# Two-layer graph network on one core: one-run picks, two-input compares, and no small reduces on VectorE

## The reference, cut to what matters

```python
# x (6250, 64), 200000 edges: src, dst (sorted), edge_attr (200000, 64), edge_weight
h = max(layernorm(x), 0)
hw = h @ W0 + b0                                   # layer 0
agg = segment_sum(edge_weight[:, None] * hw[src], dst) / (segment_sum(edge_weight, dst) + 1e-6)
x = x + relu(agg)
h = max(layernorm(x), 0)                           # layer 1
m = gelu(concat(h[src], edge_attr) @ W_msg + b_msg)
agg = segment_sum(m, dst)
x = x + gelu(((1 + eps) * h + agg) @ W_upd + b_upd)
```

## Time and profile before

| what | value |
|---|---|
| median of 3 runs | 3848.11 us |
| the profiled execution | 3829.86 us |
| its span | 3828.0 us |
| PE / DVE / ACT / POOL busy | 83% / 69% / 24% / 75% |
| chain that ended last | POOL 72%, issue 23% |

### The profile page before, as it was taken

The page is one execution under the profiler, slowest core; times in us unless marked ns, Lnnn a source line. Parts: engine busy times, 40 slices in busy tenths (PEclk is TensorE's granted clock), DMA queues, the critical chain, the costliest instruction groups (busy, mean ns, idle before and its releaser), DMA issues.

```text
span 3828.0 us, 91321 instructions
## 1 busy us (share of the span) xinstructions
PE 3159.8 (83%) x31003; PEld 3019.9 (79%) x31004; DVE 2640.0 (69%) x9401; ACT 902.6 (24%) x2966; POOL 2852.0 (75%) x2710
## 2 busy tenths in 40 slices
PE   2888888888888878878778888889888889888888
PEld 2888787788887878778777787878787888787877
DVE  6767677766667667776667676767666667676764
ACT  3222222222222222222332221222222222212121
POOL 3777777777777777777467777777777777777774
PEclk9999999999999999998789999999998989999998
DMA  2111111111111111111122222222222222222221
GB/s 83 29 29 28 28 30 29 28 28 28 28 28 30 29 28 28 30 29 28 23 57 55 55 55 54 56 54 55 55 55 54 55 55 55 55 55 55 54 55 42
DMA packets 153254, 163.39 MB, mean 43 GB/s; under 512 B 54930, under 2 KB 84430, under 8 KB 153226
## 3 DMA queue, kind: packets, MB, share of 16 engines
q0 software_dynamic: 86240, 88.48, 12.7%
q1 hardware_dynamic: 66986, 74.55, 6.7%
HBM read 157.94 MB, written 4.90 MB: 43 GB/s over the span
## 4 chain that ended last, share of the span: by engine, by line
POOL 72%; issue 23%; SPq 1%; PE 1%; POOLq 1%; DMA 1%; ACT 1%; DVE 0%; DVEq 0%
POOL rows L429 72%; PE ps L699 1%; SPq L309 1%; SPq L329 0%; POOLq L427 0%; ACT sums_sb L547 0%; DMA h_table<-h_sb 0%; POOLq L420 0%; PE ps L659 0%; SPq L302 0%; DMA p_table<-h_sb 0%; PE ps L725 0%; SPq L306 0%; DVE h_sb L814 0%; DVE h_sb L1055 0%
## 5 line engine op out<-in xcount | busy, mean ns | idle before, releaser
L429 POOL DMA_INDIRECT rows<-p_table,idx x1372 | 1441.6, 1051 | 439.4 <-issue 417.8
L627 PE MATMUL ps<-parts,pick_all 125*128 125x192 bf16 x19600 | 1717.8, 249 | 31.8 <-DVE pick_all L932 21.9
L429 POOL DMA_INDIRECT rows<-h_table,idx x1323 | 1394.5, 1054 | 426.7 <-issue 426.7
L627 PEld LDWEIGHTS ps<-parts,pick_all 125*128 125x128 bf16 x19600 | 1663.4, 99 | 43.7 <-issue 21.6
L932 DVE TENSOR_SCALAR pick_all<-src_off 125x1280 bf16<-125x1280 int16 (+1 forms) x1960 | 1323.5, 711 | 0.6
L659 PE MATMUL ps<-onehot,room 128*65 128x128 f32 (+1 forms) x6272 | 894.8, 304 | 313.1 <-ACT room L522 307.1
L659 PEld LDWEIGHTS ps<-onehot,room 128*65 128x65 f32 (+1 forms) x6272 | 793.6, 155 | 378.6 <-ACT room L522 344.9
L900 DVE TENSOR_SCALAR onehot<-iota,dw 128x128 f32<-128x128 f32 x3136 | 680.6, 288 | 33.7 <-issue 24.5
L1100 DVE TENSOR_TENSOR room<-ps,rows 128x512 f32<-128x512 f32 x196 | 135.6, 692 | 560.4 <-DMA rows<-p_table,idx 559.3
L749 PE MATMUL ps<-W1b_sb,eT 128*128 128x128 f32 x1568 | 256.7, 315 | 254.9 <-ACT eT L562 254.4
L986 DVE TENSOR_TENSOR sums_sb<-sums_sb,ps 65x128 f32 (+1 forms) x392 | 108.5, 277 | 499.4 <-PE ps L659 499.3
(11 more groups left out here) (87 smaller groups left out, 692.0 us busy)
## 6 DMA issues: line engine op xcount, KB each, us to landing
ea<-in_edge_attr_dram SPq DMA_DIRECT2D x196, 256.0 KB
rows<-p_table,idx POOLq DMA_INDIRECT x1372
rows<-h_table,idx POOLq DMA_INDIRECT x1323
src_bc<-last_src SPq DMA_DIRECT2D x196, 62.5 KB
x_sb<-in_x_dram SPq DMA_DIRECT2D x5, 312.5 KB
h_table<-h_sb SPq DMA_DIRECT2D x5, 312.5 KB
p_table<-h_sb SPq DMA_DIRECT2D x5, 312.5 KB
out_dram<-h_sb SPq DMA_DIRECT2D x5, 312.5 KB
```

Source lines behind the costliest of these rows:

```text
L429: nc.gpsimd.indirect_dma_start(out=rows[:, s, j, 0:D], out_offset=None, in_=table[:, :], in_offset=bass.IndirectOffsetOnAxis(ap=idx[:, s, ...
L627: last = nc.tensor.matmul(psG[(s + shift) % 2], pick[(s + shift) // 2 % 2][0:PN, n, at:at + P], parts[:, n, :], start=(n == 0), stop=(n == ...
```

## The change

Nothing of what is computed changes. Three things do. The picks and `src_off` get layouts in which each compare reads one run of 1280 (or 1920) elements and writes one such run. The 8 one-hots become one two-input compare with broadcast inputs, and the 5 shifts become one two-input subtraction from a table `node_k` that is written once at the start. All calls of `one_port` are gone. Waits and semaphores stay as they are.

```diff
-        node_f = sb("node_f", [PN, KN])
+        node_k = sb("node_k", [PN, KN, PE3], i16)
-        src_off = sb("src_off", [PN, KN, PE3], i16)
+        src_off = sb("src_off", [PN, KN * PE3], i16)
-        pick = [pick_all[:, 0:NK * PE3].rearrange("p (n e) -> p n e", n=NK),
-                pick_all[:, NK * PE3:].rearrange("p (n e) -> p n e", n=NK)]
+        pick = [[pick_all[:, 0:NK * w].rearrange("p (n e) -> p n e", n=NK),
+                 pick_all[:, NK * PE3:NK * (PE3 + PE2)].rearrange("p (n e) -> p n e", n=NK)] for w in (PE3, PE2)]
...
-            meta(nc.vector.tensor_copy(node_f[:, :], node_i[:, :]))
+            meta(nc.vector.tensor_copy(node_k[:, :, :], node_i[:, :].unsqueeze(2).to_broadcast([PN, KN, PE3])))
...
-            def one_port():
-                at = next(pauses)
-                nc.vector.tensor_reduce(pause[:, at:at + 1], minus_row[:, 0:2], AX.X, ALU.add)
             def onehots(slot, done):
-                for j in range(J):
-                    if j == J // 2:
-                        one_port()
-                    last = nc.vector.tensor_scalar(onehot[:, slot % 2, j, :], iota[:, :], dw[:, slot, 0, j:j + 1],
-                                                   None, ALU.is_equal)
-                last.then_inc(done, 1)
-                one_port()
+                nc.vector.tensor_tensor(onehot[:, slot % 2, :, :], iota[:, :].unsqueeze(1).to_broadcast([P, J, WIN]),
+                                        dw[:, slot, 0, :].unsqueeze(2).to_broadcast([P, J, WIN]),
+                                        ALU.is_equal).then_inc(done, 1)
...
             def offsets(layer, i, turn, q):
-                for k in range(KN):
-                    last = nc.vector.tensor_scalar(src_off[:, k, 0:w], src_bc[:, i, 0:w], node_f[:, k:k + 1], None,
-                                                   ALU.subtract)
-                last.then_inc(s_off[layer], 1)
-                one_port()
+                nc.vector.tensor_tensor(src_off[:, 0:KN * w].rearrange("p (k e) -> p k e", k=KN), src_bc[:, i, 0:w].unsqueeze(1).to_broadcast([PN, KN, w]),
+                                        node_k[:, :, 0:w], ALU.subtract).then_inc(s_off[layer], 1)
                 dve.wait_ge(s_off[layer], q + 1)
             def pick_half(layer, i, half):
                 for c in range(half * NC // 2, (half + 1) * NC // 2):
-                    if c % (NC // 2) in (2, 4):
-                        one_port()
-                    last = nc.vector.tensor_scalar(pick[i][0:PN, c * KN:(c + 1) * KN, 0:w], src_off[:, :, 0:w],
-                                                   float(c * CHUNK), None, ALU.is_equal)
+                    last = nc.vector.tensor_scalar(
+                        pick[layer][i][0:PN, c * KN:(c + 1) * KN, :].rearrange("p n e -> p (n e)"),
+                        src_off[:, 0:KN * w], float(c * CHUNK), None, ALU.is_equal)
```

More of the change, by code:

```diff
@@ L108, in two_layer_gnn @@
     CONSTS = 7
-    PAUSES = 160
     ctx = ExitStack()
@@ L186, in two_layer_gnn @@
         tick = sb("tick", [1, SLOTS])
-        pause = sb("pause", [1, PAUSES])
         ps = ctx.enter_context(nc.psum_tensor("ps", [P, 8, 512], fp32))
@@ L626, in gather @@
                 for n in range(NK):
-                    last = nc.tensor.matmul(psG[(s + shift) % 2], pick[(s + shift) // 2 % 2][0:PN, n, at:at + P],
+                    last = nc.tensor.matmul(psG[(s + shift) % 2], pick[layer][(s + shift) // 2 % 2][0:PN, n, at:at + P],
                                             parts[:, n, :], start=(n == 0), stop=(n == NK - 1))
@@ L633, in extra @@
                 for n in range(q * NK // 4, (q + 1) * NK // 4):
-                    last = nc.tensor.matmul(psX, pick[0][0:PN, n, PE2:PE3], parts[:, n, :],
+                    last = nc.tensor.matmul(psX, pick[0][0][0:PN, n, PE2:PE3], parts[:, n, :],
                                             start=(n == 0), stop=(n == NK - 1))
@@ L886, in _ @@
             nc.vector.memset(dw_tab[0:TWICE // J, LAST, 0, :], -1e6).then_inc(s_tables, 1)
-            pauses = iter(range(PAUSES))
-            def one_port():
-                at = next(pauses)
-                nc.vector.tensor_reduce(pause[:, at:at + 1], minus_row[:, 0:2], AX.X, ALU.add)
             def onehots(slot, done):
-                for j in range(J):
-                    if j == J // 2:
-                        one_port()
-                    last = nc.vector.tensor_scalar(onehot[:, slot % 2, j, :], iota[:, :], dw[:, slot, 0, j:j + 1],
-                                                   None, ALU.is_equal)
-                last.then_inc(done, 1)
-                one_port()
+                nc.vector.tensor_tensor(onehot[:, slot % 2, :, :], iota[:, :].unsqueeze(1).to_broadcast([P, J, WIN]),
+                                        dw[:, slot, 0, :].unsqueeze(2).to_broadcast([P, J, WIN]),
+                                        ALU.is_equal).then_inc(done, 1)
             def first_onehots(layer, b, s, shift):
```

## The result

The changed kernel takes 4098.1 us (median of 4 runs, 4082.75 to 4102.92), the kernel before 3848.12 beside it: 1.065 times as long, 95% interval 1.063 to 1.067. Forecast were 4088 us in a range of 3700 to 4300.

A forecast was written before the change was run, and what follows sets the result against it. The gathers on POOL bound the kernel. Surplus per body of 5.45 us (layer 0) and 5.4 (layer 1), times 49, gives 532 us instead of 292: +240, so 4070 profiled, 4088 for the median; range 3700 to 4300.

The forecast's parts named there:

- the term that moves: Gather time on POOL above an undisturbed 0.944 us, summed over both layers: from 292 us to 532, +240.
- direct, 1280: Five 1280-element compares following other VectorE work without a wait: holding a gather costs 1.85 us each.
- direct, 1920: Wide compares of layer 0 following other work without a wait: 1.9 us each, between 1.6 and 2.9.
- after a wait, 1280: 1280-element compares behind the wait on s_off: 0.3 us each for the gathers beside them.
- after a wait, 1920: Wide compares of layer 0 behind the wait on s_off: 0.3 us each for the gathers beside them.
- Released at the next boundary: Rival: two-input work ahead of compares acts as a wait, direct stretches cost 0.3 us; 3780 us; chance 0.32.
- everything holds: Rival: a gather asking during a two-input instruction enters only at the first gap; +575, 4423 us; chance 0.11.
- The layout: One run in and out makes all compares fast; fast direct stretches go from 1 to 2 a body, about 1.85 us each.
- Two-input work: One-hots and offsets, 6.4 us a body, hold gathers 0.17 us per us: 1.1 us a body, ends 0 and 2.7.
- the first rival: The case of gathers let in at the next instruction boundary: 3780 us, chance 0.32, of which 0.28 faster.
- The reduces: Removing 242 us of busy DVE off the bound; some rescued gathers in layer 0's wide stretches, included in the 1.9.
- The sign of a wrong forecast: Gathers beside direct stretches end within 0.4 us of the first compare's end; mean gather then under 1.05.

The follow-up runs named there:

- a_gap_ahead: Changed kernel plus one more VectorE wait ahead of the one-hots of each group, on the last window sum's marker: 3923.93 us, 1.021 of the kernel before.
- b_layout: Kernel before with the one-run layouts of src_off and both pick buffers alone: 4054.07 us, 1.056 of the kernel before.
- a_rows: Changed kernel with src_off in rows 2 elements apart, so every compare reads five rows and writes one run: 3850.18 us, 1.004 of the kernel before.
- b_nopause: Kernel before without the 1764 small reduces and nothing else: 3768.52 us, 0.981 of the kernel before.
- b_gap_nopause: Kernel before without the small reduces, plus a wait behind the one-hots for their own end: 3597.64 us, 0.936 of the kernel before.
- b_rows_nopause: Kernel before without the small reduces, every compare reading five separate rows and writing one run: 3595.78 us, 0.935 of the kernel before.
- b_layout_gap: Kernel before with one-run layouts, no small reduces and a wait behind the one-hots: 5356.15 us, 1.019, where TensorE bounds; rerun elsewhere 3713.44 us, 0.969.
- b_rows_gap: Kernel before without small reduces, compares from five rows into one run, wait behind the one-hots: 5373.71 us, 1.022, on the chip where TensorE bounds.

## Why the prediction was right, and where not
**The bound, the term that moves, and the sum: right.** POOL stayed the bound with 0.30 us of issue between gathers. 292 us of surplus was to become 532 and became 545. VectorE's gain of 630 us was worth nothing, as said.

**Its split: wrong in both layers, and the errors cancelled.** 267 us were forecast for layer 0 and 265 for layer 1; they are 169 and 376. I had one price for a kind of stretch. Adding up what the gathers beside each stretch took over 0.944 us gives these means:

| stretch | forecast, with its two-input part | layer 0 | layer 1 |
|---|---|---|---|
| direct, 1280 | 1.85 + 0.2 | 0.95 | 2.0 |
| direct, 1920 | 1.9 + 0.2 | 0.68 | none |
| after a wait, 1280 | 0.3 + 0.35 | 1.06 | 1.87 |
| after a wait, 1920 | 0.3 + 0.4 | 0.69 | none |

The 2.0 us of layer 1 hits the forecast by luck: it is the mean of 2.7 in the stretches without a standstill and 1.25 in those with one. So each of the two strong rivals was true somewhere. "Released at the next boundary" is layer 0, "everything holds" is what 49 direct stretches and 95 of the others in layer 1 do. What tells them apart wasn't in the forecast: whether VectorE stood still right ahead of the two-input instruction. a_gap_ahead sets that by hand and gives layer 1 the price of layer 0.

**The layout: right in kind, its split not.** Forecast as the second quick direct stretch; alone it is +224 us of surplus, 1.056. Beside the compares of direct stretches it added 143 us, beside those after a wait 89; I had put the latter at 0.6 us a body in all, and in b_layout they are 1.6. The compares came at 0.48 to 0.50 us, as scaled.

**Two-input work: undersized.** I took the rate of a few instructions of 0.82 us with gaps of 0.05 to 0.1 us between some of them, 1.1 us a body. a_rows has 3.3 with its compares slow, above even my upper end of 2.7, which let a hold reach no further than one instruction. Those rows had the gaps that the new stretches lack, which I noted only against the first rival. The durations, 1.22, 0.81 and 1.15, were right. Two 16-bit elements do go at a time: 640 more of them took 0.34 us in the offsets, 0.53 ns each, where the earlier trace rows have 0.396 us for 384 of 32 bits, 1.03 ns each.

**The reduces: wrong.** I read three of them doing nothing in the earlier trace rows and priced their going at nothing but some rescued gathers; taking them out alone took 62 us of surplus away. The 0.14 us of the earlier trace rows were off the bound and yet not free.

**What would show it.** The mean gather was to be 1.14 us and is 1.146 (3090 us over 2695). Gathers over 2.5 us were to be 150 to 190 and are 99, all in layer 1. The sign of a wrong forecast, a gather that ends within 0.4 us of the first compare's end, is there in 44 of the 97 direct stretches of layer 0, and in 42 more and in 48 of layer 1 it is missed by some 0.12 us. The mean of 1.05 that was to go with it isn't there, because layer 1 holds longer.

**Two slips in the working.** The upper end of the forecast's own range was to be 2.6 us for a direct stretch and 2 for the two-input work; with 0.6 for the stretches after a wait that is 7.8 us a body, and so 4320 us, not 4230. And the gather of 1.63 us in the earlier trace rows wasn't held to the end of the offsets: if 0.82 us are left once a gather is in, it was let in at 1003.73 - 0.82 = 1002.91, 0.70 us before that end. "Everything holds" had that one row for it.

**One instruction and no more.** The Trainium skill, "SBUF — State Buffer", section "Who interferes with whom", lets the second comer wait until the instruction of the first ends. The rows of layer 0 shown above agree, with two-input one-hots of 1.23 us and a release 0.00 us behind their end. Those of layer 1 don't: the gather shown outlasted one two-input instruction and five compares, for 2.7 us over its normal time. Where they differ the trace decides.

## What to carry to other kernels
When GpSimd's gathers are the bound, VectorE's time is free but its manner isn't: look at the spread of the gather's own duration, not at its mean or its waits. An unbroken run of two-input VectorE instructions and quick compares can hold one gather for as long as the run lasts, here up to 3.8 us. One wait for VectorE's own last result ahead of the compares took 4.5% off (b_nopause to b_gap_nopause), and a layout that keeps the compares slow took as much (b_nopause to b_rows_nopause). A small instruction in between, as the reduces of the earlier trace rows, isn't such a stop. Both best kernels, 0.935 and 0.936 of before, give VectorE more to do or more to wait for than b_nopause does.

## What the runs showed that I had not expected
**A wait that speeds up.** A standstill of 0.03 us decides between a hold of 1 us and one of 2.7. The mechanism below that is open: with a standstill ahead the gather gets in at the first boundary although the boundaries themselves overlap by the same 0.08 us. That standstills and holds go together is shown by 96 of 97 direct stretches and by two experiments; the one left had no standstill and wasn't held. Why they go together is shown by nothing here.

**Reduces that cost.** They read one input and take 0.14 us, yet without them the gathers of 1.15 to 2.5 us fell from 148 to 48. Whether they hold gathers themselves or change what the instructions around them do is open too.

**A chip where TensorE is the bound.** On it the kernel before takes 5268 us and b_layout_gap 5356, the latter elsewhere 3713. The kernel before has no trace from there; all three others that ran there have PE at 58 to 70% of the chain that ended last. From the page and the groups of b_layout_gap:
```profile
PE 69%; issue 28%; DVE 1%; ACT 1%; DMA 0%; SPq 0%; another core or an unknown queue 0%; DVEq 0%; POOL 0%
L627 PE MATMUL ps<-parts,pick_all 125*128 125x192 bf16 x19600 | 2309.6, 273 | 1255.7 <-issue 1237.0
```
In the stretch that I read (1004 to 1019 us) the matmuls of L627 stop every few instructions, mostly for 0.9 to 1.8 us, with nothing to wait for. It is 1237 us in all, where all idle time ahead of the same matmuls is 32 us in the changed kernel, at a mean granted clock of 0.80 against 0.92. What stops them isn't shown. There a change of the gathers is worth nothing or a little less than nothing: b_layout_gap gains 3% elsewhere and loses 2% there, and b_rows_gap, which joins two measures each found in a kernel at 0.935 or 0.936 elsewhere, loses 2% there. Which chip a ratio comes from belongs to it.
